# Recurrent attention in a perceiver block: the output's scale, bias and tanh as four ScalarE activations, one per sequence

## The chip, the cores and the metric

The kernel runs on one core of a Trainium2 chip. The metric is the device time of one launch in microseconds; the kernel before takes 669.55 us, the median of 3 runs (669.18 to 670.58).

The engines that matter here are TensorE (PE: matmuls, and PEld: its weight loads), VectorE (DVE) and ScalarE (ACT). Each engine works its own instructions in program order, and they meet through semaphores.

## The reference

Two layers work on 8 sequences of 32 tokens of width 128. Layer 0 is a cross attention, a windowed attention and a mixture of experts; layer 1 is an LSTM with attention at every step, four state space blocks and a routed feed-forward. The change touches only the LSTM with attention, whose recurrence is this (context: 8 sequences of 512 keys of width 128):

```python
def attend(h):
    q = h @ Wq.T
    scores = jnp.einsum('bc,bsc->bs', q, context)
    alpha = jax.nn.softmax(scores, axis=-1)
    ctx = jnp.einsum('bs,bsc->bc', alpha, context)
    return jnp.tanh(jnp.concatenate([ctx, h], axis=-1) @ Wout.T + b_out)

def step(carry, x_t):
    h, c, attn = carry
    inp = jnp.concatenate([x_t, attn], axis=-1)
    gates = inp @ W_ih.T + b_ih + h @ W_hh.T + b_hh
    i, f, g, o = jnp.split(gates, 4, axis=-1)
    c = jax.nn.sigmoid(f) * c + jax.nn.sigmoid(i) * jnp.tanh(g)
    h = jax.nn.sigmoid(o) * jnp.tanh(c)
    out = attn_out = attend(h)
    return ((h, c, attn_out), out)
```

## The kernel before

The program is written engine by engine. In the recurrent part the 8 sequences are two groups g = 0, 1 of BH = 4, and everything small is held as [128 features, 4 sequences]. `lstm_steps` (L308) calls a function `half`, of which each engine has its own, in the same order on all: one half step does `main` (attention) for one group and, for the other group, first `out` (the attention output of its step t) and then `gates` (its gates of step t + 1). There are 32 steps and 2 groups, so 64 half steps with an `out`. Nothing schedules this: the order on every engine is the order in `half`.

Keys and values have Wq and Wout folded in beforehand, so the value matmuls give the context's share of the output directly, unnormalised, in `bank[6]`. What is needed from there to the next gates:

- DVE L1171: `rz`, the reciprocal of the softmax sum, [128, 4].
- DVE L1112: `opre`, the two parts in `bank[6]` summed. L1113: times `rz`. L1115: plus `oh`, the state's share with its bias, which ACT L675 has written earlier (semaphore `oh_sb`).
- ACT L650: `a32` = tanh(`opre`), semaphore `at_32`. ACT L651: the same tanh again into `yT`, the stored outputs of all steps.
- DVE L1126 and L1128: `asp`, the output split into a 16 bit high part and the rest (`at_hi`, `at_lo`).
- PE: `output_gates` (L1611), 12 matmuls on `asp` that wait for `at_hi` and `at_lo`, and after them, for the main group, the matmul that spreads the maximum of the scores (`s_ps`), which waits for `m1` of DVE L1134.
- From there DVE L1136 (`ssum`), ACT L663 and L665 (exponentials), PE's value matmuls (`v_ps`) and DVE L1112 again. ACT L657, DVE L1143 to L1150, ACT L670 and DVE L1161 to L1164 make the new state of the other group meanwhile, and DVE L1120 and L1134 the maximum of the scores.

Matmuls of this part all go through one helper, so the trace puts them on L1591.

Of the kernel before, what the change touches and what calls it, by code (L numbers as in the profile page):

```python
# [16 lines left out]
ALU = mybir.AluOpType  # L17
ACT = mybir.ActivationFunctionType
AX = mybir.AxisListType.X
# [13 lines left out]
BH = B // 2  # L33
# [94 lines left out]
def build(nc, arr, out, upto=99):  # L128

    with ExitStack() as ctx:  # L130
# [3 lines left out]
        sem = {}  # L134
# [89 lines left out]
        yT = sb("yT", [P, B, S])  # L224
# [51 lines left out]
        bank = [psum[:, i * BANK:(i + 1) * BANK] for i in range(8)]  # L276
# [60 lines left out]
        def nth(stream, t):  # L337

            return t * 2 + (stream + 1)
# [151 lines left out]
        def _(act):  # L491
            step = Steps(act, sem["act_step"])
# [113 lines left out]
            for e in range(E + 1):  # L606
                for q in range(2):
# [3 lines left out]
                    for fc in (2 * q, 2 * q + 1):  # L611
                        half = slice((fc % 2) * TOK, (fc % 2) * TOK + TOK)
                        bias = v("b1", e * FC + fc) if e < E else v("bs1", fc)
                        ins = act.activation(T[:, 2 * (e % 2) + q, half], bank[2 * (e % 2) + q][:, half], ACT.Silu,
                                             bias=bias)
# [20 lines left out]
            for g in range(4):  # L636
                act.wait_ge(sem["l_gxps"], g + 1)
                share = bank[g][:, 0:TOK].rearrange("p (b t) -> p b t", b=B)
                for to in (gx32[:, 0:1, g * B:(g + 1) * B], gx[:, 0:1, 0, g, :]):
                    ins = act.activation(to_time(to), share, ACT.Identity, bias=gbias[:, g:g + 1],  # L640
                                         scale=lgx[:, g // 3:g // 3 + 1])
# [3 lines left out]
            def half(main=None, out=None, gates=None):  # L645
                if out:

                    g, t = out
                    act.wait_ge(sem["o_pre"], nth(g, t))
                    act.activation(a32[:, g, :], opre[:, g, :], ACT.Tanh).then_inc(sem["at_32"], 1)  # L650
                    act.activation(yT[:, g * BH:(g + 1) * BH, t], opre[:, g, :], ACT.Tanh) \  # L651
                       .then_inc(sem["y_st"], 1)
                if gates:

                    g, t = gates
                    act.wait_ge(sem["g_ps"], nth(g, t))
                    act.activation(gact[:, g, :], bank[GATES[g]][:, 0:4 * BH], ACT.Tanh, scale=lgate[:, :]) \  # L657
                       .then_inc(sem["g_act"], 1)
                if main:

                    g, t = main
                    act.wait_ge(sem["s_sum"], nth(g, t))
                    act.activation(esp[:, g, 0, :], ssum[:, g, :], ACT.Exp, scale=lexp[:, :]) \  # L663
                       .then_inc(sem["e_hi"], 1)
                    act.activation(e32[:, g, :], ssum[:, g, :], ACT.Exp, scale=lexp[:, :]) \  # L665
                       .then_inc(sem["e_32"], 1)
                if gates:
                    g, t = gates
                    act.wait_ge(sem["c_new"], nth(g, t))
                    act.activation(tanhc[:, g, :], c2[:, g, :], ACT.Tanh, scale=0.5).then_inc(sem["c_tanh"], 1)  # L670
                if main:

                    g, t = main
                    act.wait_ge(sem["oh_ps"], nth(g, t))
                    act.activation(oh[:, g, :], bank[5][:, 0:BH], ACT.Identity, bias=v("bout"), scale=loh[:, :]) \  # L675
                       .then_inc(sem["oh_sb"], 1)

            act.wait_ge(sem["l_zero"], L_ZEROED)
            lstm_steps(half)


# [84 lines left out]
        def _(dve):  # L766
            step = Steps(dve, sem["dve_step"])
# [184 lines left out]
            for j in range(NJ):  # L952

                dve.wait_ge(sem["a_score"], j + 1)
                for odd in range(2):
                    step.mark(dve.scalar_tensor_tensor(
                        out=pat(T[:, j, :], [[2 * S, AH // 2], [1, S]], odd * S),
# [9 lines left out]
            for j in range(NJ):  # L967
# [7 lines left out]
                for b in range(BT):  # L975
                    part = slice(b * S, (b + 1) * S)
                    ins = dve.transpose(aprobT[part, j, :, part], heads(T[part, 6 + j, :]))
# [87 lines left out]
            for e in range(E + 1):  # L1065
# [4 lines left out]
                for j in range(NJ):  # L1070
                    ins = (dve.scalar_tensor_tensor(out=facc[:, j, :], in0=bank[4 + e % 2][:, j * D:(j + 1) * D],
                                                       scalar=cw[:, 2, j, e:e + 1] if e < E else 0.1,
                                                       in1=facc[:, j, :], op0=ALU.mult, op1=ALU.add))
# [20 lines left out]
            def parts(t, n, k):  # L1094

                return pat(t, [[1, n], [n, k]])
# [10 lines left out]
            def half(main=None, out=None, gates=None):  # L1107
                if out:

                    g, t = out  # L1110
                    dve.wait_ge(sem["v_ps"], nth(g, t))
                    step(dve.tensor_reduce(opre[:, g, :], parts(bank[6][:, 0:1], BH, 2), AX, ALU.add))  # L1112
                    step(dve.tensor_tensor(opre[:, g, :], opre[:, g, :], rz[:, g, :], ALU.mult))  # L1113
                    dve.wait_ge(sem["oh_sb"], nth(g, t))
                    dve.tensor_tensor(opre[:, g, :], opre[:, g, :], oh[:, g, :], ALU.add).then_inc(sem["o_pre"], 1)  # L1115
                if main:

                    g, t = main
                    dve.wait_ge(sem["s_hi"], nth(g, t))
                    dve.tensor_reduce(mc[:, g, :], bank[1][:, 0:BH * KC].rearrange("p (b c) -> p b c", c=KC), AX, ALU.max) \  # L1120
                       .then_inc(sem["m_c"], 1)
                if out:

                    g, t = out
                    dve.wait_ge(sem["at_32"], nth(g, t))
                    dve.tensor_scalar(asp[:, g, 0, :], a32[:, g, :], UNIT, None, ALU.mult).then_inc(sem["at_hi"], 1)  # L1126
                    dve.wait_ge(sem["at_hi"], nth(g, t))
                    dve.scalar_tensor_tensor(out=asp[:, g, 1, :], in0=a32[:, g, :], scalar=UNIT, in1=asp[:, g, 0, :],  # L1128
                                             op0=ALU.mult, op1=ALU.subtract).then_inc(sem["at_lo"], 1)
                if main:  # L1130

                    g, t = main
                    dve.wait_ge(sem["m_t"], nth(g, t))
                    dve.tensor_reduce(m1[0:BH, g:g + 1], bank[3][0:BH, 0:P], AX, ALU.max).then_inc(sem["m_d"], 1)  # L1134
                    dve.wait_ge(sem["s_ps"], nth(g, t))
                    dve.tensor_reduce(ssum[:, g, :], pat(bank[1][:, 0:1], [[1, BH * KC], [BANK, 2], [BH * KC, 2]]),  # L1136
                                      mybir.AxisListType.XY, ALU.add).then_inc(sem["s_sum"], 1)
                if gates:

                    g, t = gates  # L1140
                    dve.wait_ge(sem["g_act"], nth(g, t))
                    i, f, o, gg = (gact[:, g, k * BH:(k + 1) * BH] for k in range(4))
                    step.mark(dve.scalar_tensor_tensor(out=fc2[:, g, :], in0=f, scalar=1.0, in1=c2[:, g, :],  # L1143
                                                       op0=ALU.add, op1=ALU.mult))
                    step.mark(dve.scalar_tensor_tensor(out=ig[:, g, :], in0=i, scalar=1.0, in1=gg,
                                                       op0=ALU.add, op1=ALU.mult))
                    step.sync()
                    dve.scalar_tensor_tensor(out=c2[:, g, :], in0=fc2[:, g, :], scalar=0.5, in1=ig[:, g, :],
                                             op0=ALU.mult, op1=ALU.add).then_inc(sem["c_new"], 1)
                    step.mark(dve.tensor_scalar(o1[:, g, :], o, 1.0, UNIT, ALU.add, ALU.mult))  # L1150
                if main:

                    g, t = main
                    dve.wait_ge(sem["e_32"], nth(g, t))
                    dve.tensor_tensor(esp[:, g, 1, :], e32[:, g, :], esp[:, g, 0, :], ALU.subtract).then_inc(sem["e_lo"], 1)
                if gates:

                    g, t = gates
                    dve.wait_ge(sem["c_tanh"], nth(g, t))
                    step.sync()  # L1160
                    dve.tensor_tensor(hsp[:, g, 0, :], o1[:, g, :], tanhc[:, g, :], ALU.mult).then_inc(sem["h_hi"], 1)  # L1161
                    step(dve.tensor_tensor(h32[:, g, :], o1[:, g, :], tanhc[:, g, :], ALU.mult))
                    dve.wait_ge(sem["h_hi"], nth(g, t))
                    dve.tensor_tensor(hsp[:, g, 1, :], h32[:, g, :], hsp[:, g, 0, :], ALU.subtract).then_inc(sem["h_lo"], 1)  # L1164
                if main:

                    g, t = main
                    dve.wait_ge(sem["z_ps"], nth(g, t))
                    step(dve.tensor_reduce(zs[:, g, :], pat(bank[4][:, 0:1], [[KC, BH], [BH * KC, 2], [1, KC]]),
                                           mybir.AxisListType.XY, ALU.add))  # L1170
                    step(dve.reciprocal(rz[:, g, :], zs[:, g, :]))  # L1171
# [773 lines left out]
```

## Time and profile before

| what | value |
| --- | --- |
| median of 3 runs | 669.55 us |
| the profiled execution's own time | 671.14 us |
| its span, first to last instruction | 669.2 us |
| mean granted TensorE clock over the span | 0.757 |
| PE, PEld, DVE, ACT busy | 83%, 63%, 70%, 46% of the span |
| recurrent part | about 221 to 447 us |
| its granted clock | 0.50 of full speed |

A profile lists for each engine when each instruction ran. Busy shares tell little of a recurrence, in which engines work in turn. What counts is the chain of work: at each instruction, what released it. The idle time before an instruction and its releaser, in brackets in the timeline, tell which engine stood and for whom.

### The profile page before, as it was taken

What the parts mean: (1) busy time and instruction counts of PE and PEld (TensorE: products, weight loads), DVE (VectorE), ACT (ScalarE), POOL (GpSimd) and SP (SyncE); (2) the same over time, 40 slices, a digit from 0 to 9 for tenths busy, and PEclk for the clock granted to TensorE, in tenths of its full rate; (3) what the DMA queues carried; (4) which work ended last, traced back from release to release, by engine and by line L of the source; (5) the groups of instructions that cost most, each with busy time, mean ns of one, the idle gap of its engine ahead of it and who ended that gap; (6) DMA issues with size and microseconds to landing.
All of it is one profiled execution on the core that took longest, in us unless ns stands there. A gap on an engine that the chain in (4) does not pass through costs nothing.

```text
span 669.2 us, 20727 instructions
## 1 busy us (share of the span) xinstructions
PE 554.7 (83%) x8469; PEld 424.9 (63%) x8469; DVE 470.1 (70%) x1830; ACT 308.5 (46%) x906; POOL 163.7 (24%) x209
## 2 busy tenths in 40 slices
PE   6968768668995699999999999966988898889847
PEld 4535543356884588888888888855656665666535
DVE  2577649956444677777777777761788998998882
ACT  3768636225565443444443444433545454555501
POOL 4255623027000000000000000003376347544700
PEclk9969979697998555555555555555888998998896
DMA  9900000010002000000000000000000000000000
GB/s 321 410 3 2 1 3 1 2 46 0 1 1 95 3 4 3 4 5 3 4 4 4 4 4 3 5 3 0 0 1 2 0 1 0 1 1 0 1 0 8
DMA packets 6255, 16.05 MB, mean 24 GB/s; under 512 B 2656, under 2 KB 3432, under 8 KB 5648
## 3 DMA queue, kind: packets, MB, share of 16 engines
q1 hardware_dynamic: 5744, 14.47, 5.9%
q8 instruction: 66, 1.08, 0.7%
q10 hardware_dynamic: 416, 0.26, 0.1%
q14 instruction: 29, 0.24, 0.1%
HBM read 14.60 MB, written 0.13 MB: 22 GB/s over the span
## 4 chain that ended last, share of the span: by engine, by line
PE 39%; DVE 33%; ACT 15%; issue 10%; POOL 2%; DMA 1%; DVEq 0%; ACTq 0%
PE bank L1684 8%; PE bank L1591 6%; PE bank L1752 6%; ACT esp L663 3%; PE bank L1542 2%; DVE ssum L1136 2%; ACT a L650 2%; ACT e L665 2%; PE bank L1529 2%; DVE w L1191 2%; DVE rz L1171 2%; DVE opre L1112 2%; DVE asp L1126 2%; DVE opre L1113 2%; DVE opre L1115 2%
## 5 line engine op out<-in xcount | busy, mean ns | idle before, releaser
L1591 PE MATMUL bank<-esp,qblk 128*128 128x1 f16 (+1 forms) x2048 | 66.5, 166 | 11.9 <-ACT esp L663 11.9
L1591 PEld LDWEIGHTS bank<-esp,qblk 128*128 128x128 f16 x2048 | 61.2, 104 | 17.2 <-ACT esp L663 17.2
L468 POOL MEMSET ctxT<- 128x128 f32 x1 | 0.3, 313 | 285.0 <-DVE xres L1178 285.0
L1591 PE MATMUL bank<-hsp,kT 128*128 128x2 f16 x2048 | 63.5, 166 | 2.0 <-DVE hsp L1164 1.9
L1591 PEld LDWEIGHTS bank<-hsp,kT 128*128 128x128 f16 x2048 | 59.5, 104 | 2.2 <-DVE hsp L1161 1.7
L650 ACT ACTIVATE a<-opre 128x4 f32<-128x4 f32 x64 | 13.1, 205 | 80.7 <-DVE opre L1115 80.7
L1204 DVE SCALAR_TENSOR_TENSOR T<-bank,bct,T 128x256 f32<-128x256 f32 x112 | 46.4, 472 | 2.2 <-PE bank L1765 2.2
L1191 DVE TENSOR_TENSOR_SCAN qblk<-ctxT,bank 128x512 f32<-128x512 f32 x32 | 37.7, 1207 | 6.0 <-PE bank L1752 5.7
L657 ACT ACTIVATE gact<-bank,lgate 128x16 f32<-128x16 f32 x64 | 17.5, 274 | 45.8 <-PE bank L1591 45.8
L1191 DVE TENSOR_TENSOR_SCAN w<-kT,bank 128x512 f32<-128x512 f32 x32 | 37.6, 1205 | 1.1 <-PE bank L1752 1.1
L1752 PE MATMUL bank<-maskb,T 128*128 128x512 f32 x64 | 37.6, 714 | 0.5 <-ACT T L735 0.5
L1591 PEld LDWEIGHTS bank<-asp,lsp 128*128 128x128 f16 x768 | 25.4, 105 | 17.1 <-DVE asp L1126 16.8
L1591 PE MATMUL bank<-hsp,lsp 128*128 128x4 f16 x984 | 35.4, 166 | 0.0
L1591 PE MATMUL bank<-asp,lsp 128*128 128x4 f16 x768 | 30.7, 168 | 5.6
L1752 PE MATMUL bank<-w,T 128*128 128x512 f32 x64 | 34.2, 650 | 0.1
L486 POOL TENSOR_TENSOR kT<-T,aneg 128x496 f32<-128x496 f32 x32 | 32.0, 1030 | 0.0
L486 POOL TENSOR_TENSOR ctxT<-T,aneg 128x496 f32<-128x496 f32 x32 | 32.0, 1031 | 0.0
L1591 PEld LDWEIGHTS bank<-hsp,lsp 128*128 128x128 f16 x984 | 31.3, 104 | 0.0
L534 ACT ACTIVATE T<-T,xneg 128x512 f32<-128x512 f32 x32 | 23.0, 718 | 10.5 <-DVE xneg L846 10.4
L414 POOL TENSOR_SCALAR T<-T,xrz 128x512 f32<-128x512 f32 x32 | 22.2, 694 | 21.3 <-DVE xrz L852 21.3
L1136 DVE TENSOR_REDUCE ssum<-bank 128x16 f32<-128x64 f32 x64 | 14.4, 225 | 18.6 <-PE bank L1591 18.6
L480 POOL TENSOR_TENSOR maskb<-cst,bct 128x512 f32<-128x512 f32 x16 | 16.1, 1040 | 44.5 <-ACT bct L726 44.5
(326 smaller groups left out, 1390.4 us busy)
## 6 DMA issues: line engine op xcount, KB each, us to landing
w<-in_w_dram SPq DMA_DIRECT2D x2, 2048.0 KB
ctxT<-in_ctxT_dram SPq DMA_DIRECT2D x8, 256.0 KB, 6.3
wqkv<-in_qkvT_dram SPq DMA_DIRECT2D x1, 1536.0 KB, 12.2
w<-in_mw_dram SPq DMA_DIRECT2D x1, 1024.0 KB, 5.0
lw<-in_lw_dram SPq DMA_DIRECT2D x1, 960.0 KB, 24.0
rows<-in_rows_dram SPq DMA_DIRECT2D x1, 772.0 KB, 9.0
wqkv<-in_fw_dram SPq DMA_DIRECT2D x1, 532.0 KB, 3.4
T<-in_mask_dram SPq DMA_DIRECT2D x1, 512.0 KB, 6.0
```

What stands on the lines that cost most here:

```text
L414: pool.tensor_scalar(x_soft(i), x_soft(i), xrz[:, i:i + 1], 0.0, ALU.mult, ALU.add).then_inc(sem["x_norm"], 1)
L486: pool.tensor_tensor(tile(c, i), pat(delta, [[0, NG], [S, BT], [1, S - 1]], ch * P + 1), pat(aneg[:, :], [[1, NG], [0, BT], [0, S - 1]], ( ...
L534: act.activation(x_soft(i), x_soft(i), ACT.Exp, scale=-1.0, bias=xneg[:, i:i + 1], accum_out=xz[:, i:i + 1]).then_inc(sem["x_exp"], 1)
L650: act.activation(a32[:, g, :], opre[:, g, :], ACT.Tanh).then_inc(sem["at_32"], 1)
L657: act.activation(gact[:, g, :], bank[GATES[g]][:, 0:4 * BH], ACT.Tanh, scale=lgate[:, :]) \
L663: act.activation(esp[:, g, 0, :], ssum[:, g, :], ACT.Exp, scale=lexp[:, :]) \
L1136: dve.tensor_reduce(ssum[:, g, :], pat(bank[1][:, 0:1], [[1, BH * KC], [BANK, 2], [BH * KC, 2]]), mybir.AxisListType.XY, ALU.add).then_inc ...
L1191: dve.tensor_tensor_scan(out=hid[q % 2][:, at], data0=decay[q % 2][:, at], data1=bank[i % 4][:, :], initial=0.0, op0=ALU.mult, op1=ALU.add ...
L1204: ins = dve.scalar_tensor_tensor(out=cacc[n % 2], in0=hT, scalar=c_n, in1=cacc[n % 2], op0=ALU.mult, op1=ALU.add)
L1591: return pe.matmul(out, lhsT, rhs, start=start, stop=stop, skip_group_check=True)
L1684: return pe.matmul(out, lhsT, rhs, start=start, stop=stop, skip_group_check=True)
L1752: pe.matmul(bank[i % 4][:, :], duT[s][:, ch * P:(ch + 1) * P], diagb[s][:, ng * 512:(ng + 1) * 512], start=True, stop=True).then_inc(sem[" ...
```

## The change

ScalarE can compute tanh(scale x in + bias) in one instruction, with scale and bias each a column of one number per partition. The scale here differs between sequences, so one activation per sequence is needed: four activations of one column each, with `rz` as scale and `oh` as bias, take the place of DVE L1113, DVE L1115 and ACT L650. The wait for `oh_sb` moves from DVE to ACT. The second tanh, into `yT`, becomes a copy of `a32`, and moves to the end of ScalarE's half step, behind `oh`; it waits for `at_32`.

```diff
@@ ScalarE, half
                     act.wait_ge(sem["o_pre"], nth(g, t))
-                    act.activation(a32[:, g, :], opre[:, g, :], ACT.Tanh).then_inc(sem["at_32"], 1)
-                    act.activation(yT[:, g * BH:(g + 1) * BH, t], opre[:, g, :], ACT.Tanh) \
-                       .then_inc(sem["y_st"], 1)
+                    act.wait_ge(sem["oh_sb"], nth(g, t))
+                    for b in range(BH):
+                        ins = act.activation(a32[:, g, b:b + 1], opre[:, g, b:b + 1], ACT.Tanh, scale=rz[:, g, b:b + 1],
+                                             bias=oh[:, g, b:b + 1])
+                    ins.then_inc(sem["at_32"], 1)
...
                        .then_inc(sem["oh_sb"], 1)
+                if out:
+                    g, t = out
+                    act.wait_ge(sem["at_32"], nth(g, t))
+                    act.activation(yT[:, g * BH:(g + 1) * BH, t], a32[:, g, :], ACT.Copy).then_inc(sem["y_st"], 1)
@@ VectorE, half
                     dve.wait_ge(sem["v_ps"], nth(g, t))
-                    step(dve.tensor_reduce(opre[:, g, :], parts(bank[6][:, 0:1], BH, 2), AX, ALU.add))
-                    step(dve.tensor_tensor(opre[:, g, :], opre[:, g, :], rz[:, g, :], ALU.mult))
-                    dve.wait_ge(sem["oh_sb"], nth(g, t))
-                    dve.tensor_tensor(opre[:, g, :], opre[:, g, :], oh[:, g, :], ALU.add).then_inc(sem["o_pre"], 1)
+                    dve.tensor_reduce(opre[:, g, :], parts(bank[6][:, 0:1], BH, 2), AX, ALU.add).then_inc(sem["o_pre"], 1)
```

ScalarE, one half step of the recurrence before, with the semaphores that each instruction waits for:

```order
L650 ACTIVATE a<-opre 128x4 [waits o_pre]
L651 ACTIVATE yT<-opre 128x4
L657 ACTIVATE gact<-bank,lgate 128x16 [waits g_ps]
L663 ACTIVATE esp<-ssum,lexp 128x16 [waits s_sum]
L665 ACTIVATE e<-ssum,lexp 128x16
L670 ACTIVATE tanhc<-c 128x4 [waits c_new]
L675 ACTIVATE oh<-bank,vec,loh 128x4 [waits oh_ps]
```

and the same half step now:

```order
L652 ACTIVATE a<-opre,oh,rz 128x1 [waits oh_sb,o_pre]
L652 ACTIVATE a<-opre,oh,rz 128x1 x3
L659 ACTIVATE gact<-bank,lgate 128x16 [waits g_ps]
L665 ACTIVATE esp<-ssum,lexp 128x16 [waits s_sum]
L667 ACTIVATE e<-ssum,lexp 128x16
L672 ACTIVATE tanhc<-c 128x4 [waits c_new]
L677 ACTIVATE oh<-bank,vec,loh 128x4 [waits oh_ps]
L682 ACTIVATE yT<-a 128x4 [waits at_32]
```

One activation of four columns is now four of one column, and the write of `yT` went from second to last.

VectorE, from the reciprocal to the sum of the scores before (`m` is `m1`, the maximum of the scores):

```order
L1171 RECIPROCAL rz<-zs 128x4 [waits dve_step]
L1112 TENSOR_REDUCE opre<-bank 128x4 [waits v_ps,dve_step]
L1113 TENSOR_TENSOR opre<-opre,rz 128x4 [waits dve_step]
L1115 TENSOR_TENSOR opre<-opre,oh 128x4 [waits oh_sb,dve_step]
L1120 TENSOR_REDUCE mc<-bank 128x4 [waits s_hi]
L1126 TENSOR_SCALAR asp<-a 128x4 [waits at_32]
L1128 SCALAR_TENSOR_TENSOR asp<-a,asp 128x4 [waits at_hi]
L1134 TENSOR_REDUCE m<-bank 4x1 [waits m_t]
L1136 TENSOR_REDUCE ssum<-bank 128x16 [waits s_ps]
```

and now:

```order
L1174 RECIPROCAL rz<-zs 128x4 [waits dve_step]
L1118 TENSOR_REDUCE opre<-bank 128x4 [waits v_ps,dve_step]
L1123 TENSOR_REDUCE mc<-bank 128x4 [waits s_hi]
L1129 TENSOR_SCALAR asp<-a 128x4 [waits at_32]
L1131 SCALAR_TENSOR_TENSOR asp<-a,asp 128x4 [waits at_hi]
L1137 TENSOR_REDUCE m<-bank 4x1 [waits m_t]
L1139 TENSOR_REDUCE ssum<-bank 128x16 [waits s_ps]
```

The product and the sum are gone; what stood behind them stands directly behind the reduction. The instructions of TensorE are the same, in the same order.

## Rows read from the trace of the kernel before

**Rows 1.** The page, the chain that ended last by engine, share of the span.

```profile
PE 39%; DVE 33%; ACT 15%; issue 10%; POOL 2%; DMA 1%; DVEq 0%; ACTq 0%
```

**Rows 2.** Busy time by stretch: the recurrent part, with the granted clock (PEclk).

```profile
228.00:446.00 218.00, 199.37 (x6082) 179.70 (x6079) 163.83 (x1127) 90.15 (x439) 0.00 (x0) 0.50 0.02 4
```

**Rows 3.** The line L650: count, duration in ns, first and last start; ScalarE's idle before.

```profile
L650 ACT ACTIVATE a<-opre x64: 205/205/206, 228.2 to 446.6; 128x4 f32<-128x4 f32 x64
its engine sat idle before it (us, times) until:
  DVE opre L1115: 80.7, 64
```

**Rows 4.** The chain in order of time, one half step: start us, us, what.

```profile
269.16 0.18 DVE opre L1112
...
269.36 0.17 DVE opre L1113
...
269.56 0.17 DVE opre L1115
...
269.75 0.21 ACT a L650
...
269.99 0.18 DVE asp L1126
```

**Rows 5.** Timeline of the half step: start us, us, what, [idle before <-releaser].

```profile
268.49 0.57 PE L1591 MATMUL bank<-esp,qblk 128*128 128x2 f16 x16
268.89 0.93 PEld L1591 LDWEIGHTS bank<-hsp,kT 128*128 128x128 f16 x32
...
269.64 0.17 DVE L1120 TENSOR_REDUCE mc<-bank 128x4 bf16<-128x16 f32 x1
...
269.86 0.27 PE L1591 MATMUL bank<-T,mc 128*4 128x128 bf16 x1
269.86 0.19 ACT L651 ACTIVATE yT<-opre 128x4 f32<-128x4 f32 x1
...
270.19 0.16 DVE L1128 SCALAR_TENSOR_TENSOR asp<-a,asp 128x4 f16<-128x4 f32 x1
270.21 0.40 PEld L1591 LDWEIGHTS bank<-asp,lsp 128*128 128x128 f16 x12 [0.28 <-DVE asp L1126]
...
270.27 0.27 DVE L1134 TENSOR_REDUCE m<-bank 4x1 bf16<-4x128 f32 x1
270.60 0.11 PEld L1591 LDWEIGHTS bank<-neg,m 128*128 128x128 bf16 x1
...
271.10 0.31 ACT L663 ACTIVATE esp<-ssum,lexp 128x16 f16<-128x16 f32 x1
...
271.31 0.29 ACT L665 ACTIVATE e<-ssum,lexp 128x16 f32<-128x16 f32 x1
...
271.51 0.20 ACT L670 ACTIVATE tanhc<-c 128x4 f32<-128x4 f32 x1
271.62 0.34 ACT L675 ACTIVATE oh<-bank,vec,loh 128x4 f32<-128x4 f32 x1
```

**Rows 6.** Groups of ScalarE by shape: out<-in count | busy us, mean ns | idle before.

```profile
L675 ACT ACTIVATE oh<-bank,vec,loh 128x4 f32<-128x4 f32 x64 | 21.6, 337 | 0.0
...
L651 ACT ACTIVATE yT<-opre 128x4 f32<-128x4 f32 x64 | 12.3, 192 | 0.0
...
L717 ACT ACTIVATE T<-T 128x256 f32<-128x256 f32 x8 | 3.3, 416 | 0.3
...
L715 ACT ACTIVATE T<-bank 128x256 f32<-128x256 f32 x8 | 3.1, 383 | 13.0 <-PE bank L1684 13.0
...
L690 ACT ACTIVATE lnv<-mv,eps 128x1 f32<-128x1 f32 x8 | 2.4, 294 | 28.8 <-DVE mv L1220 28.8
...
L691 ACT ACTIVATE rs<-lnv 128x1 f32<-128x1 f32 x8 | 1.6, 202 | 0.3
```

**Rows 7.** Timeline behind the last half step: PE's turn of the stored outputs.

```profile
446.94 0.29 PEld L1678 LDWEIGHTS bank<-cst,yT 128*128 128x128 f32 x2 [1.15 <-ACT yT L651]
```

## The prediction

> **What bounds the kernel now.** The first view is the page's chain of work [rows 1]: PE holds 39% of it, DVE 33% and ACT 15%, so no engine alone is the bound; stages follow each other. The changed stage has its own row in the busy times by stretch [rows 2]: 218 us, PE's own records sum to 199.37 us, and the granted clock is 0.50, the lower of TensorE's two levels (1.2 GHz). The reader is to see that a longer stall of PE here can't lower its clock further. L650 runs 64 times between 228.2 and 446.6 us, each time after a wait for DVE L1115 [rows 3]: the half step takes (446.6 - 228.2) / 63 = 3.467 us.
>
> Next, the chain in order of time through one half step [rows 4]: reduction at 269.16, product at 269.36, sum at 269.56, tanh at 269.75, first split at 269.99. All five are on it, and from the start of the reduction to the start of the split is 0.83 us. The timeline [rows 5] shows who stands behind: PE idles 0.28 us for `asp` before its 12 gate matmuls, and behind them in its queue wait the score matmul at 270.60, everything of the next gates, and the value matmuls. DVE's L1134 also stands behind the splits (270.27, right after L1128 at 270.19). So the softmax of one group and the gates of the other both hang on `at_32`, and there is no slack between `at_32` and the next reduction: the stage's time moves one for one with it.
>
> **The change: what goes.** Two DVE instructions. The product costs its pitch, 269.36 to 269.56, 0.20 us, and the sum about the same [rows 4]. Then ACT L650 itself, 0.205 us [rows 3]. In the path of 0.83 us these are 0.20 + 0.20 + 0.205; what stays is the reduction (0.167 us and about 0.03 to the consumer, 0.20 in all, the pitch 269.16 to 269.36) and the way from the tanh's end to the split, 269.99 - 269.75 - 0.205 = 0.035 us.
>
> **What comes.** Four activations 128x1 from `opre` to `a32`, each with a scale and a bias read from a column. None like it stands in the trace, so I build it from rows.
> - One column, no such operand: 202 ns; one column, one operand (bias): 294 ns (L691, L690) [rows 6]. An operand costs 92 ns, so two give 294 + 92 = 386 ns for one that waited.
> - An activation that directly follows another is shorter by 205 - 192 = 13 ns (L650, L651, same shape) [rows 3, 6]: 373 ns.
> - The only one with two operands and few columns is L675: 337 ns, 4 columns, from PSUM [rows 6]. From PSUM is cheaper: 383 against 416 ns at 256 columns (L715, L717), 33 ns. L675 from SBUF would be 370 ns. The two ways meet at 370 ns for a follower, and I take 0.370 us, and 0.383 for the first.
> - Overlap of neighbours: L650 starts at 269.75 and L651 at 269.86, 0.11 for 0.205 of duration; L663 to L665 0.21 for 0.308; L665 to L670 0.20 for 0.291; L670 to L675 0.11 for 0.205 [rows 3 to 6]. It is always about 0.095 us, and the operand's time is inside the duration and not overlapped. So the pitches are 0.288, 0.275 and 0.275.
>
> From the reduction's start to the split's: 0.20 + (0.288 + 0.275 + 0.275) + 0.370 + 0.035 = 1.443 us, against 0.83. That is +0.61 us in each half step.
>
> The Trainium skill, "ScalarE: Activation LUTs", section "What ACT_TABLE_LOAD costs", gives an activation 186 ns plus 0.833 ns a column, 93 ns for each column operand, and 93 ns of overlap back to back. The rows above agree on both (92 and 95 ns); the price of two operands is what no row shows alone. By the skill's page an estimate for one of the four is 373 ns with a pitch of 280 ns, and the path 0.20 + 3 x 0.28 + 0.373 + 0.035 = 1.448 us, 0.62 us over 0.83; the sum below would be some 0.4 us more. Its table of rules for kernel authors, by which additions and products belong on VectorE, speaks against this change.
>
> **Edits at nothing.** The copy into `yT` now follows `oh`. It would start about 0.24 us behind L675's start (271.62) and end near 272.05, while ScalarE's next tanh starts a half step behind 269.75, at 273.2 [rows 5]; without that cover it would cost a pitch of 0.11 us. Its old place (269.86) was hidden as well: ScalarE stood idle until the gates afterwards. `oh_sb` is there long before: L675 ends at 271.62 + 0.34, over a microsecond before the next tanh. A second semaphore to wait for on ACT may cost up to about 0.05 us, the gap between the first split's end (269.99 + 0.17) and PE's weights (270.21) [rows 4, 5], which is the longest handover in the half step; I take 0, since DVE's sum waited for two semaphores as well and still followed the product at the usual 0.20. DVE's L1120 (269.64) can now run earlier, but PE couldn't use it: its 32 score weights last until 268.89 + 0.93 = 269.82, and the matmul of `mc` starts at 269.86 [rows 5]. L1134 stands behind the splits in any case, so DVE's freed 0.4 us become idle time.
>
> **The sum.** 64 half steps x 0.613 = 39.2 us. At the end PE's turn waits for `yT` [rows 7]: before, that write ended 0.11 + 0.192 = 0.30 us behind the tanh's start, 0.10 behind its end; now it starts some 0.04 behind the end of the fourth tanh and takes 0.20, so it ends 0.24 behind it. That is 0.14 us on top of the 0.613 already counted. In all +39.3 us: span 669.2 to 708.5, that execution 671.14 to 710.4. It lies 1.6 us above the median of the runs, 669.55; for a median I predict 669.55 + 39.3 = 708.9 us.
>
> **Bounds.** Low: each of the four takes only L675's 335 ns (less 2 columns) with its overlap kept, pitch 0.242: 0.235 + 3 x 0.242 + 0.335 = 1.296, +0.466, x 64 = 29.8, 699.4 us. High: all four at 386 ns, pitch 0.291, and the second wait 0.05: 0.235 + 0.873 + 0.386 + 0.05 = 1.544, +0.714, x 64 = 45.7, 715.3 us.
>
> **Rivals.**
> 1. *No overlap among the four*, because they write neighbouring columns of one tile: 0.235 + 0.383 + 3 x 0.370 = 1.728, +0.90, x 64 = 57.5: 727 us. Against it: all four pairs above overlap, one of them of the same shape and input. 5%.
> 2. *Operands are fetched ahead between equal instructions*, so the pitch is that of L650 to L651, 0.11, with the last at 0.370: 0.235 + 0.33 + 0.370 = 0.935, +0.105, x 64 = 6.7: 676 us. Against it: L663 and L665 have the same operand `lexp`, and their pitch is still 0.21 with 16 columns. 5%.
> 3. *Faster*: the operands cost nothing at all while the engine waits for `o_pre`, in the four too; duration 0.192 and pitch 0.11 give 0.235 + 0.33 + 0.192 = 0.757, -0.073, x 64 = -4.7: 664.9 us. The place is between the reduction and `at_hi`; it decides when three pitches and the last duration come under 0.595 us. L690 waited for DVE and still showed 92 ns more than L691, so 2%.
> 4. *PE or another chain hides part of it*: if `at_32` weren't what PE waits for, the loss would shrink by the slack. PE's 0.28 us of idle before `asp` is waiting for this very chain, not slack, and adds to it. A hidden share of a quarter would give 699; this lies in the range. 5%.
>
> **How the numbers follow.** Forecast 83%, rivals 5, 5, 2 and 5%. The range goes from the low to the high bound, 699 to 716 us, and leaves out rivals 1 to 3 and a little of the forecast's own. Within 0.2% (1.3 us, about what a measurement of this kernel tells from no change): 2%, a near miss between rivals 2 and 3; faster 2%; slower 96%.
>
> **What would show it.** In the profile after: the one-column tanh 256 times, mean near 373 ns, starts 0.275 us apart; 1.44 us from the reduction on `opre` to the first split on `asp`; PE's idle before `asp` up from 0.28 to about 0.89 us; half step 4.08 us and the recurrent part some 39 us longer; clock still 0.50; other stages as long as before. A pitch of 0.11 or of 0.37, a shorter wait of PE than 0.89, or another stage that moved would make it wrong.

## The result and the profile after

The changed kernel takes 708.86 us, the median of 4 runs (707.82 to 709.59), against 669.37 us for the kernel before in the same comparison (median of 4). The ratio is 1.0586, 95% interval 1.0552 to 1.0619: 37 to 41 us slower. The profiled execution took 709.39 us, with a span of 707.2 us.

The page of the changed kernel: the chain that ended last, by engine and by line. One new entry leads it, the one-column tanh with 11% of the span; ScalarE's share rose from 15% to 23%, VectorE's fell from 33% to 28% [rows 1].

```profile
PE 37%; DVE 28%; ACT 23%; issue 9%; POOL 2%; DMA 1%; DVEq 0%; ACTq 0%
ACT a L652 11%; PE bank L1687 7%; PE bank L1594 6%; PE bank L1755 5%; ACT esp L665 3%; PE bank L1545 2%; DVE ssum L1139 2%; ACT e L667 2%; PE bank L1532 2%; DVE rz L1174 2%; DVE asp L1129 2%; DVE opre L1118 2%; DVE w L1194 2%; DVE hsp L1167 1%; DVE hsp L1164 1%
```

The line of the tanh in the changed kernel (count, duration in ns, first and last start, who waited), then the line of the first split. The tanh answers to [rows 3].

```profile
L652 ACT ACTIVATE a<-opre,oh,rz x256: 370/372/387, 228.3 to 486.2; 128x1 f32<-128x1 f32 x128
...
  DVE opre L1118: 49.1, 64
...
  DVE asp L1129: 59.5, 64
```

```profile
L1129 DVE TENSOR_SCALAR asp<-a x64: 169/170/171, 229.6 to 486.6; 128x4 f16<-128x4 f32 x64
```

The splits run from 229.6 to 486.6 us, so a half step takes 257.0 / 63 = 4.079 us; before it was 3.467 us. One such half step in the changed kernel's timeline, beside [rows 4, 5]:

```profile
272.92 0.17 DVE L1118 TENSOR_REDUCE opre<-bank 128x4 f32<-128x8 f32 x1
273.12 1.22 ACT L652 ACTIVATE a<-opre,oh,rz 128x1 f32<-128x1 f32 x4 [0.74 <-DVE opre L1118]
273.28 0.17 DVE L1123 TENSOR_REDUCE mc<-bank 128x4 bf16<-128x16 f32 x1 [0.19 <-PE bank L1594]
273.60 0.08 PEld L1594 LDWEIGHTS bank<-T,mc 128*4 128x4 bf16 x1
...
274.38 0.17 DVE L1129 TENSOR_SCALAR asp<-a 128x4 f16<-128x4 f32 x1 [0.92 <-ACT a L652]
...
274.60 0.40 PEld L1594 LDWEIGHTS bank<-asp,lsp 128*128 128x128 f16 x12 [0.92 <-DVE asp L1129]
```

From the reduction's start to the split's start is 274.38 - 272.92 = 1.46 us where it was 0.83. The four tanh fill 1.22 us of it. VectorE stands 0.92 us before the split and TensorE's weights 0.92 us before the gates, where they stood 0.18 to 0.19 and 0.28. The new idle time on both engines is one and the same delay: TensorE waits for VectorE's split, and VectorE for the fourth tanh.

The granted clock of the part stayed at 0.50. Last, busy times by stretch behind the recurrent part, of the kernel before and then of the changed one (length; PE, PEld, DVE, ACT, POOL busy; clock, DMA):

```profile
447.00:669.00 222.00, 183.27 (x902) 123.73 (x902) 170.30 (x331) 98.05 (x226) 96.57 (x99) 0.87 0.01 1
```

```profile
487.00:707.00 220.00, 180.96 (x902) 121.71 (x902) 170.11 (x331) 98.07 (x226) 96.62 (x99) 0.89 0.01 1
```

The stretch with the same 902 matmuls took 2 us less, at a granted clock of 0.89 in place of 0.87.

### The profile page after: what moved, and what is told of

Its sections match the earlier page's. It is cut to its first block, busy times and chain, and to the rows that moved or that the text cites. A ratio compares the mean times of both kernels' runs of the same rounds, so it can differ in the third digit from the quotient of the medians.

```text
span 707.2 us, 20791 instructions
## 1 busy us (share of the span) xinstructions
PE 551.2 (78%) x8469; PEld 423.2 (60%) x8469; DVE 454.7 (64%) x1702; ACT 373.9 (53%) x1098; POOL 163.8 (23%) x209
## 4 chain that ended last, share of the span: by engine, by line
PE 37%; DVE 28%; ACT 23%; issue 9%; POOL 2%; DMA 1%; DVEq 0%; ACTq 0%
ACT a L652 11%; PE bank L1687 7%; PE bank L1594 6%; PE bank L1755 5%; ACT esp L665 3%; PE bank L1545 2%; DVE ssum L1139 2%; ACT e L667 2%; PE bank L1532 2%; DVE rz L1174 2%; DVE asp L1129 2%; DVE opre L1118 2%; DVE w L1194 2%; DVE hsp L1167 1%; DVE hsp L1164 1%
## 5 line engine op out<-in xcount | busy, mean ns | idle before, releaser
L652 ACT ACTIVATE a<-opre,oh,rz 128x1 f32<-128x1 f32 x256 | 78.0, 375 | 49.1 <-DVE opre L1118 49.1
L1129 DVE TENSOR_SCALAR asp<-a 128x4 f16<-128x4 f32 x64 | 10.9, 170 | 59.5 <-ACT a L652 59.5
L1755 PE MATMUL bank<-maskb,T 128*128 128x512 f32 x64 | 36.0, 686 | 0.6 <-ACT T L741 0.5
```

The lines of the kernel that those rows point to most:

```text
L652: ins = act.activation(a32[:, g, b:b + 1], opre[:, g, b:b + 1], ACT.Tanh, scale=rz[:, g, b:b + 1], bias=oh[:, g, b:b + 1])
L1755: pe.matmul(bank[i % 4][:, :], duT[s][:, ch * P:(ch + 1) * P], diagb[s][:, ng * 512:(ng + 1) * 512], start=True, stop=True).then_inc(sem[" ...
```

## The experiments

The theory: the loss is the number of activations times what each occupies ScalarE, its duration (about 190 ns, and about 92 ns more for each column operand) less the 0.095 us in which neighbours overlap; nothing else in the change matters. The main rivals: the moved copy is part of the loss; operands or overlap behave differently among the four.

**The copy alone**, on the kernel before:

```diff
-                    act.activation(yT[:, g * BH:(g + 1) * BH, t], opre[:, g, :], ACT.Tanh) \
-                       .then_inc(sem["y_st"], 1)
...
+                if out:
+                    g, t = out
+                    act.wait_ge(sem["at_32"], nth(g, t))
+                    act.activation(yT[:, g * BH:(g + 1) * BH, t], a32[:, g, :], ACT.Copy).then_inc(sem["y_st"], 1)
```

> Only the copy part of the change: product, sum and the one tanh of four columns stay as before; the second tanh into yT becomes a copy of a32 behind oh. Theory (the copy is hidden in ScalarE's idle time, all of the loss is the four tanh): within 0.3% of before, ratio 0.997 to 1.003, path from reduction to first split still 0.83 us. Rival (the later copy holds up ScalarE's next tanh or gates by its pitch of 0.11 us): + 64 x 0.11 = 7 us, ratio 1.010.

Measured: ratio 1.001, interval 0.9992 to 1.0028. Its splits run from 229.8 to 448.0 us, 3.463 us a half step, as before. The copy costs nothing there.

**The changed kernel with the copy in the old place**, directly behind the four tanh:

```diff
                     ins.then_inc(sem["at_32"], 1)
+                    act.wait_ge(sem["at_32"], nth(g, t))
+                    act.activation(yT[:, g * BH:(g + 1) * BH, t], a32[:, g, :], ACT.Copy).then_inc(sem["y_st"], 1)
...
-                if out:
-                    g, t = out
-                    act.wait_ge(sem["at_32"], nth(g, t))
-                    act.activation(yT[:, g * BH:(g + 1) * BH, t], a32[:, g, :], ACT.Copy).then_inc(sem["y_st"], 1)
```

> The changed kernel with the copy into yT directly behind the four tanh, its old place. Theory: hidden there as well, since ScalarE stands 0.78 us idle before the gates: 709 us, ratio to before 1.059, and a few tenths of a us less at the very end. Rival (the place matters): the copy holds the gates' tanh up by its 0.2 us, + 13 us.

Measured: 709.66 us, ratio 1.0576 (1.0559 to 1.0593), no different from the changed kernel. The few tenths that I expected at the very end aren't there: the last half step has nothing between the tanh and the copy in either kernel, and the last copy ends 0.24 us behind the fourth tanh in both (here 486.80 + 0.21 = 487.01 against 485.55 + 1.22 = 486.77).

**Four plain tanh**, on the kernel before: product and sum stay, the tanh becomes four without column operands, and the copy into `yT` goes behind `oh` as in the change.

```diff
-                    act.activation(a32[:, g, :], opre[:, g, :], ACT.Tanh).then_inc(sem["at_32"], 1)
...
+                    for b in range(BH):
+                        ins = act.activation(a32[:, g, b:b + 1], opre[:, g, b:b + 1], ACT.Tanh)
+                    ins.then_inc(sem["at_32"], 1)
...
```

> Product and sum stay on VectorE; the tanh is four activations of one column without column operands (and the copy as in the change). Theory (each activation pays its own duration less 0.095 us): pitches 0.107, 0.094, 0.094, last 0.189; path 0.60 + 0.295 + 0.189 + 0.035 = 1.12 us, + 0.29 a half step, + 18.5 us, 688 us, ratio 1.028. Rival (one activation's fixed cost is shared by neighbours and only the operands cost): below + 5 us.

Measured: 688.2 us, ratio 1.0258 (1.0227 to 1.0289), 17.6 us more. Three rows of its timeline, ScalarE and VectorE:

```profile
268.94 0.17 DVE L1116 TENSOR_REDUCE opre<-bank 128x4 f32<-128x8 f32 x1
```

```profile
269.53 0.48 ACT L651 ACTIVATE a<-opre 128x1 f32<-128x1 f32 x4 [1.19 <-DVE opre L1119]
```

```profile
270.05 0.17 DVE L1130 TENSOR_SCALAR asp<-a 128x4 f16<-128x4 f32 x1 [0.46 <-ACT a L651]
```

The path is 1.11 us, and the four fill 0.48 us at 191 ns each: a pitch of (0.48 - 0.19) / 3 = 0.097 us. Splitting alone, with no operand, makes the path 0.28 us longer, and the half step by (464.6 - 228.9) / 63 - 3.465 = 0.276 us. The rival, a fixed cost shared by neighbours, falls.

**Half of the change**: the product stays on VectorE, the sum becomes the bias. The excerpt is against the kernel before; the loop over the sequences, the wait for `oh_sb` and the copy are as in the change.

```diff
-                    step(dve.tensor_tensor(opre[:, g, :], opre[:, g, :], rz[:, g, :], ALU.mult))
-                    dve.wait_ge(sem["oh_sb"], nth(g, t))
-                    dve.tensor_tensor(opre[:, g, :], opre[:, g, :], oh[:, g, :], ALU.add).then_inc(sem["o_pre"], 1)
+                    dve.tensor_tensor(opre[:, g, :], opre[:, g, :], rz[:, g, :], ALU.mult).then_inc(sem["o_pre"], 1)
...
+                        ins = act.activation(a32[:, g, b:b + 1], opre[:, g, b:b + 1], ACT.Tanh, bias=oh[:, g, b:b + 1])
```

> Half of the change: the product stays on VectorE, the sum becomes the bias of four activations of one column (one column operand each; the copy as in the change). Theory (each operand costs 0.092 us in each of the four): pitches 0.20, 0.187, 0.187, last 0.28; path 0.40 + 0.574 + 0.28 + 0.035 = 1.29 us, + 0.46, + 29.4 us, 699 us, ratio 1.044. Rival (operands are free behind the first one): one 0.29 and three pitches of 0.10, path 1.02, + 12 us, 681 us.

Measured: 698.96 us, ratio 1.0427 (1.0395 to 1.0459), 28.4 us more. ScalarE's row, and then the group of these activations with its mean:

```profile
270.81 0.85 ACT L652 ACTIVATE a<-opre,oh 128x1 f32<-128x1 f32 x4 [0.95 <-DVE opre L1118]
```

```profile
L652 ACT ACTIVATE a<-opre,oh 128x1 f32<-128x1 f32 x256 | 54.4, 282 | 62.4 <-DVE opre L1118 62.4
```

Pitch (0.85 - 0.28) / 3 = 0.19 us. With the runs before and after it this is a ladder with one rung per operand: mean 191, 282 and 375 ns; pitch 0.097, 0.19 and 0.283 us. Each operand costs 91 to 93 ns in the duration and 93 ns in the pitch. The rival of free operands falls.

**Two activations of two columns**, with the operands of the first sequence of each pair. The second sequence's own scale and bias are left out, so this kernel serves for its time alone:

```diff
-                    for b in range(BH):
-                        ins = act.activation(a32[:, g, b:b + 1], opre[:, g, b:b + 1], ACT.Tanh, scale=rz[:, g, b:b + 1],
+                    for b in (0, 2):
+                        ins = act.activation(a32[:, g, b:b + 2], opre[:, g, b:b + 2], ACT.Tanh, scale=rz[:, g, b:b + 1],
```

> The changed kernel with two activations of two columns each instead of four of one (each pair takes the operands of its first sequence, so that part of the computation is wrong). Theory (the loss is per activation): path 0.20 + 0.288 + 0.37 + 0.035 = 0.89 us, + 0.065 a half step, + 4 us, 673.5 us, ratio 1.006. Rival (the loss is in the operands' columns or elements, not in the count): near the changed kernel's 709 us.

Measured: 674.64 us, ratio 1.0068 (1.0052 to 1.0083), against 1.006 expected. Its splits run from 228.8 to 451.2 us, 3.530 us a half step, 0.065 more than the 218.3 / 63 = 3.465 us between the splits of the kernel before.

```profile
270.36 0.67 ACT L652 ACTIVATE a<-opre,oh,rz 128x2 f32<-128x2 f32 x2 [0.75 <-DVE opre L1118]
```

**One activation of four columns**, everything else as changed. It takes the first sequence's scale and bias for all four and leaves out the other three, so it too serves for its time alone:

```diff
-                    for b in range(BH):
-                        ins = act.activation(a32[:, g, b:b + 1], opre[:, g, b:b + 1], ACT.Tanh, scale=rz[:, g, b:b + 1],
-                                             bias=oh[:, g, b:b + 1])
-                    ins.then_inc(sem["at_32"], 1)
+                    act.activation(a32[:, g, :], opre[:, g, :], ACT.Tanh, scale=rz[:, g, 0:1],
+                                   bias=oh[:, g, 0:1]).then_inc(sem["at_32"], 1)
```

> The changed kernel with one activation of four columns with the scale and bias of the group's first sequence for all four (that part of the computation is wrong). VectorE's product and sum stay away. Theory: path 0.20 + 0.386 + 0.035 = 0.62 us, 0.21 less than before; but the maximum's reduction can't start before the transposing matmul has ended, 0.12 us earlier than before at best, so of 0.21 about 0.12 to 0.14 us count: - 8 to - 9 us, 661 us, ratio 0.987. Rival (nothing caps it): - 13.4 us, 656 us, ratio 0.980. Rival (removing VectorE's two operations was worth nothing on the path): + 10 us.

Measured: 661.14 us, ratio 0.9857 (0.983 to 0.9885), - 9.4 us. So VectorE's two operations were worth taking away; it is the count of four that turns the gain into a loss. The half step is 3.335 us (splits from 228.5 to 438.6), 0.13 less, while the path from 271.35 to 271.97 is 0.62 us, 0.21 less. Two thirds count. The timeline of this kernel:

```profile
271.97 0.17 DVE L1127 TENSOR_SCALAR asp<-a 128x4 f16<-128x4 f32 x1
...
272.07 0.27 PE L1592 MATMUL bank<-T,mc 128*4 128x128 bf16 x1
272.18 0.16 DVE L1129 SCALAR_TENSOR_TENSOR asp<-a,asp 128x4 f16<-128x4 f32 x1
...
272.27 0.48 PE L1592 MATMUL bank<-asp,lsp 128*128 128x4 f16 x12
272.37 0.28 DVE L1135 TENSOR_REDUCE m<-bank 4x1 bf16<-4x128 f32 x1
...
272.71 0.20 PE L1592 MATMUL bank<-neg,m 128*128 128x16 bf16 x1
```

As expected, the maximum's reduction (272.37) starts when its matmul ends (272.34) and no longer 0.08 us behind the second split (272.18). TensorE no longer stands idle before the gates; the matmul behind them that spreads the maximum (`neg,m`) still waits for this reduction and starts 0.06 us behind its end (272.65). So the maximum is the cap, as expected. From the second split to the reduction it is 0.19 us in these rows and 0.15 in the median of the half steps, 0.07 more than 0.08: of 0.21 us 0.14 are left, and 0.13 were measured.

**A version that beats both.** The sum can leave the path in another way, with no operand on ScalarE: with C = `oh` times the softmax sum, the output is tanh(`rz` x (A + B + C)), and C is made before the reciprocal, while TensorE still multiplies the values. VectorE writes C/2 twice into `bank[4]`, so that one reduction over two banks adds all four parts:

```diff
-                    step(dve.tensor_reduce(opre[:, g, :], parts(bank[6][:, 0:1], BH, 2), AX, ALU.add))
-                    step(dve.tensor_tensor(opre[:, g, :], opre[:, g, :], rz[:, g, :], ALU.mult))
-                    dve.wait_ge(sem["oh_sb"], nth(g, t))
-                    dve.tensor_tensor(opre[:, g, :], opre[:, g, :], oh[:, g, :], ALU.add).then_inc(sem["o_pre"], 1)
+                    dve.wait_ge(sem["dve_step"], share_at[0])
+                    step(dve.tensor_reduce(opre[:, g, :], pat(bank[4][:, 128:129], [[1, BH], [2 * BANK - 128, 2], [BH, 2]]),
+                                           mybir.AxisListType.XY, ALU.add))
+                    dve.tensor_tensor(opre[:, g, :], opre[:, g, :], rz[:, g, :], ALU.mult).then_inc(sem["o_pre"], 1)
...
-                    step(dve.reciprocal(rz[:, g, :], zs[:, g, :]))
...
+                    dve.wait_ge(sem["oh_sb"], nth(g, t))
+                    step.mark(dve.scalar_tensor_tensor(
+                        out=bank[4][:, 128:128 + 2 * BH].rearrange("p (k b) -> p k b", k=2),
+                        in0=pat(oh[:, g, :], [[0, 2], [1, BH]]), scalar=0.5, in1=pat(zs[:, g, :], [[0, 2], [1, BH]]),
+                        op0=ALU.mult, op1=ALU.mult))
+                    share_at[0] = step.n
+                    step.mark(dve.reciprocal(rz[:, g, :], zs[:, g, :]))
```

> Another way to take the sum off the path: VectorE multiplies oh by the softmax sum before the reciprocal (in halves, twice, into a PSUM bank free at that time), and the reduction adds these to the two parts; then the product and the one tanh of four columns. No ScalarE operand. Theory: one VectorE pitch of 0.20 us goes from the path; the maximum's reduction caps what counts at about 0.13 us: - 8 us, 661 us, ratio 0.988. Rival (no cap): - 12.8 us, ratio 0.981. Rival (the extra operation before the reduction delays it by 0.2 us, because VectorE and not the value matmuls set its start): 0 us.

Measured: 661.08 us, ratio 0.9869 (0.9853 to 0.9884): about 9 us faster than the kernel before (9.4 by the medians, 8.8 by the ratio). The half step is (437.7 - 227.6) / 63 = 3.335 us, again 0.13 less although 0.19 left the path. The extra instruction isn't free. From the reduction of the softmax sum (`zs`) to that of the output, before and then here, it takes 0.03 us more (0.475 and 0.503 in the medians):

```profile
268.68 0.19 DVE L1169 TENSOR_REDUCE zs<-bank 128x4 f32<-128x32 f32 x1
268.91 0.18 DVE L1171 RECIPROCAL rz<-zs 128x4 f32<-128x4 f32 x1
269.16 0.17 DVE L1112 TENSOR_REDUCE opre<-bank 128x4 f32<-128x8 f32 x1
```

```profile
269.96 0.19 DVE L1169 TENSOR_REDUCE zs<-bank 128x4 f32<-128x32 f32 x1
270.19 0.17 DVE L1172 SCALAR_TENSOR_TENSOR bank<-oh,zs 128x8 f32<-128x8 f32 x1
270.27 0.17 DVE L1177 RECIPROCAL rz<-zs 128x4 f32<-128x4 f32 x1
270.47 0.17 DVE L1113 TENSOR_REDUCE opre<-bank 128x4 f32<-128x16 f32 x1
```

The chain of work through one half step of this kernel:

```profile
268.93 0.32 ACT esp L663
269.24 0.05 issue
269.29 2.68 PE bank L1598 x79
271.96 0.02 issue
271.99 0.23 DVE ssum L1136
```

By this view TensorE runs 79 matmuls in a row for 2.68 us, and only the score sum and the exponential stand between two such runs. But the records of neighbouring matmuls overlap (one of the gates' lasts 0.17 us and twelve together 0.48), so a wait of 0.1 us between two of them is counted as TensorE's work. The timeline of the same half step shows such a wait:

```profile
271.11 0.27 PE L1598 MATMUL bank<-T,mc 128*4 128x128 bf16 x1
271.31 0.16 DVE L1128 SCALAR_TENSOR_TENSOR asp<-a,asp 128x4 f16<-128x4 f32 x1
...
271.33 0.48 PE L1598 MATMUL bank<-asp,lsp 128*128 128x4 f16 x12
271.42 0.28 DVE L1134 TENSOR_REDUCE m<-bank 4x1 bf16<-4x128 f32 x1
...
271.75 0.20 PE L1598 MATMUL bank<-neg,m 128*128 128x16 bf16 x1
```

`neg,m` waits for the maximum's reduction and starts 0.05 us behind its end (271.70), as before; it starts 0.42 us after the first gate matmul, where 0.32 would do (the run below). So the path over the tanh and the splits is still the one that ends last. The reduction starts 0.11 us behind the second split and not 0.08, held by the matmul that turns the maxima (it ends at 271.38). The sum closes: of 0.19 us the extra instruction takes 0.03 and the maximum 0.02 to 0.03, and 0.14 are left where 0.13 were measured.

**The same with the maxima turned earlier** on TensorE, after 10 of the 16 second score matmuls. The function holds the wait and the matmul that stood behind the scores:

```diff
                     for i in range(BH * KC):
+                        if k and i == 10:
+                            turn_max()
                         at = (g * BH * KC + i) * P
...
+                def turn_max():
+                    pe.wait_ge(sem["m_c"], nth(g, t))
+                    mm(bank[3][0:BH, 0:P], mc[:, g, :], identb, start=True, stop=True).then_inc(sem["m_t"], 1)
...
-                pe.wait_ge(sem["m_c"], nth(g, t))
-                mm(bank[3][0:BH, 0:P], mc[:, g, :], identb, start=True, stop=True).then_inc(sem["m_t"], 1)
```

> The same, and TensorE turns the maxima after 10 of the 16 second score matmuls instead of behind them. Theory (the turn was the cap): path to the gates and to the score sum both 0.20 us shorter, - 12.8 us, 656.5 us, ratio 0.981. Rival (the cap isn't there or lies elsewhere): same as the kernel with three parts alone.

Measured: 660.69 us, ratio 0.9857 (0.9838 to 0.9877), not to be told from the one above, where I expected 656.5. In the timeline of this kernel the maximum's reduction is no longer held (it starts at 270.29, again 0.08 us behind the split at 270.21), and `neg,m` starts 0.32 us after the first gate matmul (270.30, 270.62), where it was 0.42. And yet the half step only went from 3.335 to 3.319 us, because the early turn opened another wait:

```profile
269.09 0.83 PE L1598 MATMUL bank<-hsp,kT 128*128 128x2 f16 x26
...
269.69 0.18 DVE L1120 TENSOR_REDUCE mc<-bank 128x4 bf16<-128x16 f32 x1
...
269.92 0.08 PEld L1598 LDWEIGHTS bank<-T,mc 128*4 128x4 bf16 x1
269.92 0.27 PE L1598 MATMUL bank<-T,mc 128*4 128x128 bf16 x1
```

The turning matmul starts 0.05 us behind the end of VectorE's reduction (269.87) and 0.17 us behind the start of the last score matmul (269.09 + 0.83 - 0.17 = 269.75); in the version above that is 0.10 us (270.19 + 0.99 - 0.17 = 271.01, 271.11). `neg,m` starts 0.06 us behind the end of the maximum's reduction (270.56) and directly behind the gate matmuls, so TensorE, with the new wait in it, and the path now end within 0.01 us of each other. My expectation failed in its size: I had put on the maximum all of the 0.06 us that hadn't counted in the version above, but 0.03 of them were the extra instruction.

**The turn after 14 of the 16**, otherwise the same:

> Three parts in the reduction, and the maxima turned after 14 of the 16 second score matmuls, not 10. With 10, TensorE stood 0.09 us for the maxima and then worked back to back up to the score sum. Theory (TensorE's own work from the value matmuls to the score sum is now the bound, plus that stall): the stall goes, but VectorE's splits and the maximum's reduction end at nearly the same moment, so of 0.09 us at most 0.05 counts: between 657.5 and 661 us, ratio 0.981 to 0.986. Rival (the early turn is worth its full 0.07 us once the stall is gone): 656 us or less, ratio 0.979.

Measured: 659.6 us, ratio 0.9849 (0.9818 to 0.988), half step (437.7 - 229.5) / 63 = 3.305 us. This is within the expected band and above the rival's 656 us. The wait for VectorE is gone (from the last score matmul's start to the turn it is 0.10 us again), and TensorE waits for the maximum again: `neg,m` starts 0.39 us after the first gate matmul (269.62, 270.01) and 0.05 us behind the end of the reduction, which starts 0.08 us behind the second split (269.60, 269.68, 0.27 long). By the traces each of the two steps took some 0.015 us from the half step, 1 us in all each; the timed runs can't tell the three versions apart. The chain through this one:

```profile
270.24 0.24 DVE ssum L1136
270.48 0.02 issue
270.50 0.32 ACT esp L663
270.82 0.05 issue
270.86 2.64 PE bank L1598 x79
```

So these 2.64 us don't show TensorE's own work as the bound: within them it waits for the path. Some 0.05 to 0.07 us less on the path and TensorE would be the last one; that is an estimate from 0.39 against 0.32, and no run tests it.

## Why the prediction was right

Point by point, by its own steps:

- **One path, no slack.** Shown. The path grew by 1.46 - 0.83 = 0.63 us and the half step by 4.079 - 3.467 = 0.61 us. The run with two pairs has + 0.065 us in the half step against + 0.063 by the sum for its path.
- **What goes.** Two VectorE pitches and one tanh, 0.605 us. With one wide activation the path was 0.62 us against 0.621 by the same prices (0.20 + 0.386 + 0.035). On the gaining side the prediction's "one for one" wouldn't have held: only 0.13 of 0.21 us counted, as the maximum of the scores came to hold the path by 0.07 us. On the losing side nothing of the kind can help.
- **What comes.** A duration of 0.370 us for a follower was forecast, and the median was 372 ns, from 370 to 387. The pitches were forecast at 0.288, 0.275 and 0.275, 0.838 us for three; measured 1.22 - 0.372 = 0.85 us. The term was 0.01 us too small, since the neighbours' overlap is 0.09 here and not 0.095. Both of the ways that led to 0.370, one operand's price doubled and the row of `oh` from PSUM, came within 3 ns; the ladder confirms the first, and no run tests the price of PSUM by itself. The estimate of 373 ns and a pitch of 0.28 us, worked out from the Trainium skill, "ScalarE: Activation LUTs", section "What ACT_TABLE_LOAD costs", agrees with the trace (372 ns, 0.283 us).
- **The copy at nothing.** Shown by two runs, once alone and once in the old place. In the changed kernel it ran in ScalarE's idle time. At the very end it ended 486.64 + 0.21 = 486.85, 0.24 us behind the last tanh's end at 486.61, as forecast.
- **The second wait at nothing.** The tanh starts 0.20 us behind the reduction's start (272.92, 273.12), the pitch from before; no cost.
- **TensorE's idle time** was forecast at 0.89 us and is 0.92 us. The clock stayed at 0.50.
- **The sum.** Forecast 708.9 us, measured 708.86 us. That close is partly luck: the interval alone is four microseconds wide, and from the first split to the last the time grew by 257.0 - 218.3 = 38.7 us, with the first half step's 0.6 and the tail's 0.14 that is 39.4 against 39.3 forecast, but the span grew only by 38.0. The forecast that other stages would be unchanged failed by 2 us: the part behind the recurrence was that much shorter in this execution, at a slightly higher granted clock, and the part ahead of it half a microsecond longer. Nothing ties this to the change: from the last split to the end of the span the kernel before takes 222.4 us, the changed one 220.6, and the kernel with the copy alone 219.5, and over all eleven traces, in which nothing differs there, it goes from 219.4 to 223.0 us. The prediction had named a stage that moved as a sign of being wrong; it had no row for how much one moves by itself. (Its 39.3 is a rounding slip as well: 39.23 and 0.14 are 39.4.)

Of the rivals, no overlap (727 us) and shared operands (676 us) are ruled out by the ladder of 191, 282 and 375 ns, and the faster one by the same rows. Slack of another chain (the fourth) is ruled out by the half step, which grew by as much as the path to within 0.02 us.

The step that failed stands in the experiments, not in the prediction: with three parts I took the maximum for the whole of what didn't count. It held the path by 0.02 to 0.03 us, and lifting it gave 0.016; as much was the price of the extra instruction, which I had at nothing.

## What to carry to other kernels

A scale and a bias that ScalarE takes from columns pay only if one instruction can use them for all its elements: then the two cost 0.18 us here (388 ns against 205) and take the place of 0.40 us on VectorE. Where they differ between columns the activation has to be split, and on tiny tiles the count of instructions is the price: here four of 0.28 us each took the place of one of 0.2 us and two VectorE steps of 0.2 us, and even without operands the split alone lost more than one of the saved steps gave.

To shorten such a chain, look for algebra that moves an operation ahead of the late operand. tanh(r (a + b) + o) became tanh(r (a + b + o z)) with z = 1/r known early: one step of 0.19 us left the path and one more instruction ahead of the reduction cost 0.03, for about 9 us.

Price a saving and a loss differently: a longer step on a path without slack counts in full, a shorter one only until another wait ends last. That wait needs no idle time in the profile: where records overlap, it shows only in the starts of the instructions.

## What the runs showed of the hardware

- ScalarE's cost of a column operand is a clean term: 191, 282 and 375 ns (means of 256) for a one-column tanh with none, one and two; and 388 ns for four columns with two that waited. The second operand costs as much as the first, and neighbouring equal instructions that take their operands from the same tiles save nothing but the usual overlap.
- Four activations that write neighbouring columns of one tile overlap as those on separate tiles do: 0.09 us.
- Matmuls of 2 columns start 0.027 us apart here when nothing holds them (32 in 0.99 us, at a granted clock of 0.50), while each record lasts 0.17 us; TensorE's wait of 0.10 us for the maximum stands in no idle time of the profile.
- VectorE's reduction across two PSUM banks, 16 elements a partition for 8, took 175 ns in place of 167.
